# Image mix with its matrix as stationary, inside the value stage, turned through DRAM

## What is computed

```
xa = x.reshape(B * T, 1, H, W)          # after a group norm, 4 columns of W a group
xn = _inorm(xa, norm1_w, norm1_b)
k, q = (_fno_layer(xn, cw, sw, H // 2, W // 2) for cw, sw in ((Kcw, Ksw), (Qcw, Qsw)))
v = _fno_layer(xn, Vcw, Vsw, H, W)      # 32 heads: spectral part + pointwise skip
p_attn = softmax(scores(q, k))          # over the 32 images of a batch
av = einsum('bnts,bnsk->bntk', p_attn, v)
p = _fno_layer(av, Pcw, Psw, H, W)      # back to one head: spectral part + skip
a = _inorm(p + xa, attn_w, attn_b)
```

## Time and profile before

| what | us |
|---|---|
| median of 3 runs | 1873.72 (1869.31 to 1873.76) |
| the profiled execution | 1878.36 |
| its span, first to last instruction | 1876.6 |
| PE busy in the span | 1649.6 |
| DVE busy | 1484.6 |
| ACT busy | 1033.4 |
| POOL busy | 596.7 |

### The profile page before, as it was taken

How to read it: one execution, slowest core, us unless ns; L and a number is a source line. 1 busy time by engine, 2 the same in 40 slices (tenths; PEclk the granted TensorE clock), 3 DMA queues, 4 the chain that set the end, 5 groups by cost and what they waited for, 6 DMA issues and landing times.

```text
span 1876.6 us, 29918 instructions
## 1 busy us (share of the span) xinstructions
PE 1649.6 (88%) x11143; PEld 1018.5 (54%) x11143; DVE 1484.6 (79%) x2631; ACT 1033.4 (55%) x1544; POOL 596.7 (32%) x676
## 2 busy tenths in 40 slices
PE   7776878899889989389999999999999999999683
PEld 7751222699789989144444544445444454444342
DVE  5779999537766679889987998879988788884873
ACT  4379000133636155367777766677766776677620
POOL 2335878300256025424760130002280004000633
PEclk9897999999899999599999999999999999999897
DMA  6660363000000024000120021000132012000892
GB/s 159 252 163 23 93 151 87 8 1 1 1 1 2 1 72 116 3 1 1 23 57 1 13 34 34 12 1 23 24 80 57 1 57 62 7 12 19 296 377 104
DMA packets 132429, 114.03 MB, mean 61 GB/s; under 512 B 40384, under 2 KB 109376, under 8 KB 131744
## 3 DMA queue, kind: packets, MB, share of 16 engines
q1 hardware_dynamic: 128352, 108.00, 20.2%
q0 software_dynamic: 1536, 3.08, 0.5%
q10 hardware_dynamic: 2400, 1.03, 0.3%
HBM read 83.99 MB, written 21.88 MB: 56 GB/s over the span
## 4 chain that ended last, share of the span: by engine, by line
PE 67%; DVE 17%; issue 7%; ACT 6%; DMA 2%; POOL 1%; SPq 0%; POOLq 0%; DVEq 0%; ACTq 0%
PE PS L561 5%; PE PS L563 5%; PE PS L562 5%; PE PS L582 5%; PE PS L583 5%; PE PS L584 5%; PE PS L1467 5%; PE PS L1540 4%; PE PS L1549 4%; PE PS L543 4%; DVE U L1251 4%; PE PS L1700 3%; ACT Z L829 2%; DVE U L1308 2%; PE PS L531 2%
## 5 line engine op out<-in xcount | busy, mean ns | idle before, releaser
L826 ACT ACTIVATE Z<-PS,MI 128x1024 f32<-128x1024 f32 (+2 forms) x288 | 300.3, 1043 | 250.7 <-PE PS L563 221.3
L1033 DVE TENSOR_TENSOR DB<-Z 128x1024 f16<-128x1024 f32 (+2 forms) x288 | 333.4, 1158 | 100.9 <-ACT Z L829 51.7
L1013 DVE TENSOR_REDUCE MI<-PS 128x1 f32<-128x512 f32 (+2 forms) x576 | 356.8, 640 | 36.8 <-PE PS L543 20.2
L829 ACT ACTIVATE Z<-PS,MI 128x1024 f16<-128x1024 f32 (+2 forms) x288 | 298.5, 1037 | 0.0
L739 POOL TENSOR_SCALAR U<-U,Z 128x128 f32<-128x128 f32 x128 | 71.8, 576 | 323.0 <-DVE MI L1063 323.0
L756 POOL TENSOR_SCALAR Z<-U,Z 128x128 f32<-128x128 f32 x104 | 66.6, 652 | 338.9 <-PE PS L584 236.4
L1263 POOL TENSOR_TENSOR U<-A,U 128x1408 f32<-128x1408 f32 x45 | 142.3, 3209 | 42.6 <-PE PS L1672 22.1
L1251 DVE TENSOR_TENSOR U<-A,PS 128x1408 f32<-128x1408 f32 x99 | 152.9, 1616 | 3.3 <-PE PS L1666 3.2
L1672 PE MATMUL PS<-U 128*32 128x352 f32 x1152 | 112.7, 495 | 0.1
L582 PE MATMUL PS<-Z,A 128*128 128x512 f16 (+3 forms) x288 | 104.3, 362 | 6.2 <-ACT CST L837 6.2
L582 PE MATMUL PS<-Z,V 128*128 128x512 f16 (+3 forms) x288 | 104.0, 361 | 4.0 <-ACT CST L837 4.0
(11 more groups left out here) (437 smaller groups left out, 3595.1 us busy)
## 6 DMA issues: line engine op xcount, KB each, us to landing
V<-in_L_ffn_weight SPq DMA_DIRECT2D x16, 1024.0 KB, 11.4
U<-in_L_ffn_weight SPq DMA_DIRECT2D x14, 1024.0 KB, 14.6
A<-x_planes SPq DMA_DIRECT2D x24, 528.0 KB, 9.4
U<-in_x SPq DMA_DIRECT2D x16, 512.0 KB, 4.3
V<-in_x SPq DMA_DIRECT2D x4, 2048.0 KB, 14.0
Z<-in_x SPq DMA_DIRECT2D x16, 512.0 KB, 4.7
out<-U SPq DMA_DIRECT2D x16, 512.0 KB, 3.4
token_rows<-U SPq DMA_DIRECT2D x16, 512.0 KB, 3.9
```

Source lines behind the costliest of these rows:

```text
L826: act.activation(EX32[u % 2][:, 0:w], s, ACT.Exp, scale=SCALE / (QUP * KUP), bias=pb).then_inc(sem("ex_ev"), 1)
L829: act.activation(EHI[u % 3][:, 0:w], s, ACT.Exp, scale=SCALE / (QUP * KUP), bias=pb).then_inc(sem("hi_ev"), 1)
L1013: dve.tensor_reduce(bm[:, g % 2, t, k:k + 1], PS[:, 4 + chunk_no[c] % 2, 0:w], AX.X, ALU.max).then_inc(sem("ch_ev"), 1)
L1033: dve.tensor_tensor(ELO[u % 3][:, 0:w], EX32[u % 2][:, 0:w], EHI[u % 3][:, 0:w], ALU.subtract).then_inc(sem("lo_ev"), 1)
```

## The change

- The norm of `V` takes four columns (one group of the group norm, which has one scale) in an instruction.
- The planes of the value stage have one set of banks, 0 to 2. A row's first value matmuls wait for the sums of the row before it (`zv_ev` >= r), and VectorE makes these sums after group 0 of the new row instead of group 1.
- The image mix moves into the value stage. After each of the first 32 groups of VectorE, TensorE makes one `mix(g)`: `Mt` is stationary, 512 columns of `V` move, the result (image on the partition) goes to bank 3, 4 or 5. ScalarE copies it back over the same columns of `V`, and after every fourth copy issues a DMA of 2048 columns to the DRAM tensor `mixed`.
- SP loads `mixed` into `U` with h on the partition, 16 loads of eight images, three in flight, after all writes have landed and all value matmuls are done.
- TensorE's fold waits for `mx_ev` and `zv_ev` alone; the copies into `U` are gone. VectorE's additions in the first inverse wait for the load of their images. The semaphores of a later load of `x` take the new names, with counts shifted.

```diff
--- before.py
+++ after.py
...
@@ -1238,6 +1239,11 @@
                 dve.wait_ge(sem("fin_mm"), n + 1)
                 dve.tensor_tensor(token[q][k], token[q][k], PS[:, n % 8, 0:D], ALU.add).then_inc(sem("fin_ready"), 1)
 
+        MIX_BANKS = (3, 4, 5)
+        NMIX = 32
+        mixes_after = [min(d + 1, NMIX) for d in range(len(VALUES_DVE))]
+        row_ends = [sum(NDVS[:r + 1]) for r in range(NR)]
+
         def value_products(dve, d):
 
             r, g = VALUES_DVE[d]
@@ -1403,6 +1409,15 @@
                                  io[f"L0_conv_{n}"].rearrange("a b k x c -> (a b k) (x c)")).then_inc(sem("mw_in"), 16)
                 sp.dma_start(wrow[:, i], io[f"L0_conv_{n}"][0, :, :, 0, :]).then_inc(sem("mw_in"), 16)
 
+            sp.wait_ge(sem("mix_out"), 16 * NMIX // 4)
+            sp.wait_ge(sem("v_dve"), 3 * len(VALUES_DVE))
+            sp.wait_ge(sem("v_pool"), 3 * len(VALUES_POOL))
+            mix_nat = mix_dram.rearrange("n (h w) -> h n w", w=W)
+            for c in range(16):
+                if c >= 3:
+                    sp.wait_ge(sem(f"images_in{c % 3}"), 16 * (c // 3))
+                sp.dma_start(U[:, 8 * c:8 * c + 8, :], mix_nat[:, 8 * c:8 * c + 8, :]).then_inc(sem(f"images_in{c % 3}"), 16)
+
             sp.wait_ge(sem("tr_mm"), 3 * NTR)
             for i, n in enumerate("qkv"):
                 sp.dma_start(WN3[:, i, :], io[f"L1_attn_W{n}"]).then_inc(sem("l1w_in"), 16)
...
@@ -1669,37 +1684,37 @@
             def values(y, r, g, q, stop):
                 for b in range(B):
                     s = slice(32 * b, 32 * b + 32)
-                    mm = pe.matmul(PS[s, 3 * (r % 2) + q, 0:MR], PT[:, g, s], y[:, b, q, :], start=(g == 0), stop=stop)
+                    mm = pe.matmul(PS[s, q, 0:MR], PT[:, g, s], y[:, b, q, :], start=(g == 0), stop=stop)
                 return mm
+
+            def mix(g):
+                if g == 0:
+                    pe.wait_ge(sem("once_dve"), MADE["mt"])
+                    pe.wait_ge(sem("once_act"), BY_ACT_ONCE["xg"])
+                if g >= 3:
+                    pe.wait_ge(sem("mx_ev"), g - 2)
+                pe.matmul(PS[:, MIX_BANKS[g % 3], :], Mt, V[:, 512 * g:512 * g + 512], start=True, stop=True).then_inc(sem("mx_mm"), 1)
 
             spread(0)
             spread(1)
             p = -1
             for d, (r, g) in enumerate(VALUES_DVE):
                 p += g in POOL_BEHIND[NDVS[r]]
-                if g == 0 and r >= 2:
-                    pe.wait_ge(sem("zv_ev"), r - 1)
                 for q in range(3):
                     i = 3 * d + q
                     pe.wait_ge(sem("y_dve"), i + 1)
                     if i + 2 < 3 * len(VALUES_DVE):
                         spread(i + 2)
+                    if g == q == 0 and r:
+                        pe.wait_ge(sem("zv_ev"), r)
                     values(YB[d % 2], r, g, q, g == NDVS[r] - 1 and g not in POOL_BEHIND[NDVS[r]]).then_inc(sem("v_dve"), 1)
                     if g in POOL_BEHIND[NDVS[r]]:
                         pe.wait_ge(sem("y_pool"), 3 * p + q + 1)
                         values(YB[2], r, VALUES_POOL[p][1], q, g == NDVS[r] - 1).then_inc(sem("v_pool"), 1)
-            pe.wait_ge(sem("once_dve"), MADE["mt"])
-            pe.wait_ge(sem("once_act"), BY_ACT_ONCE["xg"])
-            xg = V[:].rearrange("p (h w) -> p h w", w=W)
-            for g in range(32):
-                if g >= 4:
-                    emptied(pe, "mx_ev", g - 4)
-                elif g == 0:
-                    pe.wait_ge(sem("zv_ev"), NR)
-                for j in range(4):
-                    mm = pe.matmul(PS[:, g % 4, 128 * j:128 * j + 128], xg[:, :, 4 * g + j], Mt, start=True, stop=True)
-                mm.then_inc(sem("mx_mm"), 1)
-            all_emptied(pe, "mx_ev", 1, 32)
+                for m in range(mixes_after[d - 1] if d else 0, mixes_after[d]):
+                    mix(m)
+            pe.wait_ge(sem("mx_ev"), NMIX)
+            pe.wait_ge(sem("zv_ev"), NR)
             pe.wait_ge(sem("once_dve"), MADE["wf"])
             for i in range(2):
                 for c in range(2):
@@ -1771,13 +1786,14 @@
 
             act.wait_ge(sem("once_dve"), MADE["rim"])
             act.wait_ge(sem("xi_in"), 64)
-            Vc = V[:].rearrange("p (h w) -> p w h", w=W)
+            Vc = V[:].rearrange("p (h w) -> p h w", w=W)
 
 
             def norm_columns(a, b):
 
-                for w in range(a, b):
-                    ins = act.activation(Vc[:, w, :], Vc[:, w, :], ACT.Identity, scale=rim[:, w:w + 1], bias=cim[:, w:w + 1])
+                for w in range(a, b, GW):
+                    x = Vc[:, :, w:w + GW]
+                    ins = act.activation(x, x, ACT.Identity, scale=rim[:, w:w + 1], bias=cim[:, w:w + 1])
                 return ins
 
             norm_columns(0, 96)
@@ -1789,14 +1805,25 @@
                 act.activation(PT[:, 4 * h:4 * h + 4, :].rearrange("p n s -> p (n s)"), PS[:, 2 + h, :], ACT.Copy).then_inc(sem("pt_ev"), 1)
             norm_columns(104, W).then_inc(sem("once_act"), 1)
             act.wait_ge(sem("x_out"), 48)
-            for r in range(NR):
-                act.wait_ge(sem("v_dve"), 3 * sum(NDVS[:r + 1]))
+
+            def first_plane(r):
+                act.wait_ge(sem("v_dve"), 3 * row_ends[r])
                 act.wait_ge(sem("v_pool"), 3 * sum(NQ - n for n in NDVS[:r + 1]))
-                act.activation(Z[:, 2, MR * r:MR * r + MR], PS[:, 3 * (r % 2), 0:MR], ACT.Copy).then_inc(sem("k1_ready"), 1)
-            Um = U[:].rearrange("p n w -> p w n")
-            for g in range(1, 32, 2):
+                act.activation(Z[:, 2, MR * r:MR * r + MR], PS[:, 0, 0:MR], ACT.Copy).then_inc(sem("k1_ready"), 1)
+
+            def mixed_out(g):
                 act.wait_ge(sem("mx_mm"), g + 1)
-                act.activation(Um[:, 4 * g:4 * g + 4, :], PS[:, g % 4, :].rearrange("p (w n) -> p w n", w=4), ACT.Copy).then_inc(sem("mx_ev1"), 1)
+                act.activation(V[:, 512 * g:512 * g + 512], PS[:, MIX_BANKS[g % 3], :], ACT.Copy).then_inc(sem("mx_ev"), 1)
+                if g % 4 == 3:
+                    act.wait_ge(sem("mx_ev"), g + 1)
+                    s = slice(512 * (g - 3), 512 * (g + 1))
+                    act.dma_start(mix_dram[:, s], V[:, s]).then_inc(sem("mix_out"), 16)
+
+            for d in range(len(VALUES_DVE)):
+                if d + 1 in row_ends:
+                    first_plane(row_ends.index(d + 1))
+                for m in range(mixes_after[d - 1] if d else 0, mixes_after[d]):
+                    mixed_out(m)
 
             def weigh_modes(layer):
 
@@ -2048,13 +2075,13 @@
                 dve.wait_ge(sem("k1_ready"), r + 1)
                 if r == 0:
                     dve.wait_ge(sem("x_out"), 48)
-                dve.tensor_tensor(Z[:, 0, m], Z[:, 2, m], PS[:, 3 * (r % 2) + 2, 0:MR], ALU.subtract)
-                later(dve.tensor_tensor(Z[:, 1, m], Z[:, 2, m], PS[:, 3 * (r % 2) + 1, 0:MR], ALU.add))
+                dve.tensor_tensor(Z[:, 0, m], Z[:, 2, m], PS[:, 2, 0:MR], ALU.subtract)
+                later(dve.tensor_tensor(Z[:, 1, m], Z[:, 2, m], PS[:, 1, 0:MR], ALU.add))
                 dve.tensor_scalar(Z[:, 2, m], Z[:, 0, m], -1.0, None, ALU.mult).then_inc(sem("zv_ev"), 1)
 
             for d, (r, g) in enumerate(VALUES_DVE):
                 value_products(dve, d)
-                if g == 1 and r:
+                if g == 0 and r:
                     value_sums(r - 1)
             value_sums(NR - 1)
 
@@ -2065,11 +2092,7 @@
             later(dve.tensor_tensor(wrow[:, :, neg, 0], wrow[:, :, neg, 0], wrow[:, :, pos, 0], ALU.add))
             later(dve.tensor_tensor(wrow[:, :, neg, 1], wrow[:, :, neg, 1], wrow[:, :, pos, 1], ALU.subtract))
             dve.memset(wrow[:, :, 0:32, :], 0.0).then_inc(sem("once_dve"), 1)
-            Um = U[:].rearrange("p n w -> p w n")
             dve.wait_ge(sem("z_ready"), 1)
-            for g in range(0, 32, 2):
-                dve.wait_ge(sem("mx_mm"), g + 1)
-                dve.tensor_copy(Um[:, 4 * g:4 * g + 4, :], PS[:, g % 4, :].rearrange("p (w n) -> p w n", w=4)).then_inc(sem("mx_ev0"), 1)
 
             def transposed_evacs(layer):
                 for g in range(0, NTR, 2):
@@ -2104,9 +2127,10 @@
             dve.wait_ge(sem("once_mm"), ONCE["fold"])
             later(dve.tensor_copy(WR[:, :, 0, :], PS[:, 5, 0:4].rearrange("p (l c) -> p l c", l=2)))
             dve.tensor_scalar(WN, WR[:, :, :, 1], -1.0, None, ALU.mult).then_inc(sem("once_dve"), 1)
-            all_emptied(dve, "mx_ev", 1, 32)
             transposed_evacs(0)
             for k in range(NIM):
+                if k % 2 == 0:
+                    dve.wait_ge(sem(f"images_in{k // 2 % 3}"), 16 * (k // 6 + 1))
                 dve.wait_ge(sem("i2_mm"), k + 1)
                 u = U[:, 4 * k:4 * k + 4, :]
                 dve.tensor_tensor(u, u, PS[:, 4 + k % 4, :].rearrange("p (n w) -> p n w", w=W), ALU.add).then_inc(sem("i2_ev"), 1)
```

(5 more changed lines are left out.)

## The result

| what | before | after |
|---|---|---|
| median, us | 1873.74 (1869.31 to 1875.64) | 1841.40 (1839.99 to 1842.94) |
| ratio, 95% interval | | 0.9831 [0.9811, 0.9851] |
| profiled execution, us | 1878.36 | 1840.46 |
| its span, us | 1876.6 | 1838.3 |
| value stage, first product to last sum, us | 169.0 | 195.3 |

The kernel became 32.3 us faster; 36.2 were forecast. The mix left the path as the prediction has it, and the value stage paid more for it than was forecast.

What follows compares the result with a forecast made beforehand. Stages follow one another: TensorE bounds the image mix and first inverse, VectorE the value stage. Terms -56.6 + 4 + 16.4 = -36.2 us give 1837.5 us against the median; range 1824 to 1857.

Steps and rivals of the forecast that it cites:

- mix off the path: Between last sum and fold: without the image mix the fold starts at 351.44 instead of 408.07, -56.6 us.
- mixes inside rows: Value stage: two mixes close together around a long group show about 0.37 us, twice in six rows, +4 us.
- row ends, beyond the 13.9 before: Five row ends: one plane set makes TensorE wait for VectorE's sums; 30.3 us against 13.9, +16.4 us.
- ways of the data, norm of V: Writes to DRAM, loads back and ScalarE's four-column norm steps: all hidden, 0 us.
- A mix at 0.86 us: TensorE in the value stage: one 512-column mix takes 0.86 us, or 1.08 if weight loads show.
- The 0.37 us behind a long group: Value stage: what shows when two mixes lie close together around a long group, twice in each of six rows.
- the hold: Row ends before rows 2 and 4: POOL's product holds up VectorE's last sum, 2.8 us more at each.
- Which clock at the row ends: TensorE behind the waits: low clock taken at all five ends; if only half fell, some 4 us cheaper.
- The data: Loads of mixed images into U: three in flight, 2.8 us each, hidden by 11 us at the narrowest.
- A: Value stage: TensorE catches up and keeps its clock, stage stays 169 us, mix goes under it; 1817 us, chance 0.10.
- B: Value stage: TensorE becomes the bound through weight loads, POOL's loads and low clock; 1855.5 us, chance 0.17.
- C: First inverse: images come back late from DRAM, one by one at 9.4 us a load; 1918 us, chance 0.06.

Runs made afterwards that it cites:

- run 6: Changed kernel with the 16 loads of mixed images one at a time instead of three in flight; 1841.89 us.
- run 2: Changed kernel with the 32 mixes placed elsewhere: four in TensorE's wait at each of five row ends, ten inside rows, two after the last row; 1820.65 us.
- run 4: Changed kernel with each mix matmul made twice, same operands and bank; 1866.13 us.
- run 5: Changed kernel with 16 matmuls of 128 columns, results unused, in TensorE's wait at each of five row ends; 1833.76 us.
- run 1: Kernel before with only one set of plane banks, its wait, and the sums after group 0; image mix in its old place; 1889.35 us.
- run 7: Changed kernel with the norm of V in 128 single columns as before; 1846.54 us.
- run 3: Changed kernel with VectorE's last sum made from PSUM, plane 2 minus plane 0, instead of a negated SBUF copy; 1837.15 us.

## Why the prediction was right, and where not

**The mix leaves the path: right.** The fold stands 1.14 us behind the last sum (375.88 to 377.02); 1.1 was forecast.

**The sum by its terms.** From the first product to the fold are 226.8 us before (181.30 to 408.07) and 196.4 after (180.58 to 377.02): -30.3 by the change, where the prediction has -36.2.

| term | predicted | measured |
|---|---|---|
| mix off the path | -56.6 | -56.6 |
| mixes inside rows | +4 | +6.2 |
| row ends, beyond the 13.9 before | +16.4 | +20.0 |
| ways of the data, norm of V | 0 | 0 |

The two middle terms were mis-sized, by 2.2 and 3.6 us; that is the whole miss up to the fold (but for 0.1 of rounding). The first is as large in run 6 (6.3 us), which has the same value stage. The second is not: from first product to fold run 6 takes 191.7 us instead of 196.4, and the difference lies at its row ends, 29.0 us instead of 33.9, where the clock fell less. That is 15.1 us beyond the 13.9, so the 16.4 of the forecast lies inside the scatter of this term. The median fell by 32.3 us, between the 30.3 of this execution and the 35.1 of run 6.

The profiled executions differ by 37.9 us, and some 7 of it lie behind the last addition into `U`: 1397.8 us from its end to the end of the span before, 1390.6 after, between 1390.1 and 1396.5 in the eight experiments. That is work which no edit here touches, but for the names of some semaphores, so I take it as scatter; this isn't shown. So it is luck that the profiled execution came so near to its forecast (1840.46 against 1842): these 7 us made up for the terms that were taken too low.

**A mix at 0.86 us: too low.** It takes 0.97 (187.17 to 188.14). The prediction had both ends, 0.86 and 1.08, and chose the lower since `Mt` lies contiguous. Back to back, four take 3.60 us (run 2); without the 0.16 by which a mix's row reaches past the next start (1.13 against 0.97) that is 0.86 each, as for a second mix with the same matrix (run 4). So 0.11 us more shows once for each mix that stands alone between other shapes, where I had weighed none or two; that it is a weight load is argued, not shown. The 0.37 us behind a long group became 0.54; it shows 11 times, and 0.25 once: 6.2.

**Row ends: the mechanism right, two steps too cheap.** The wait has the five places and the releaser that were forecast, and is somewhat shorter: 3.5 us at three ends and 5.5 with POOL at two, where about 4 and 7 were named. At the odd end above the first product is late by 4.39 us; the prediction's parts for it (1.24 + 0.14 + 2.51 + 0.51) make 4.4. Then I took 0.73 and about 0.6 us for the second product and the mix; the first is from the earlier trace rows, where the clock came back within the second batch. Here the second batch is slow to its end, and 1.23 and 1.00 show. The 1.00 is no price of the clock: it stands behind all three odd ends of run 5 too, where both batches are at full speed. It is the mix behind a long group that began late. At the even ends the hold is 2.58 us (2.8 taken), but the low clock lasts through three steps and into the mix: 1.73 us late there at the one, 1.15 at the other, instead of 0.7. That the hold came so near is in part luck: it is what is left of POOL's product at that moment, and the same two ends show 0.43 and 2.97 us in run 1, 0.99 and 0.96 in run 2. Sums: 6.6, 7.8, 5.6, 7.2 and 6.8 against 5.7, 6.6, 5.7, 6.6 and 5.7.

**Which clock at the row ends.** All five at the low one was right for this execution, and the trace agrees with the rule that I named from the Trainium skill ("TensorE: Matmul & The Clock Gate", Part 1) in direction. But it isn't certain for the odd ends: behind 3.5 us of idling the first sixteen matmuls ran slow at three of three odd ends in after, and at one of three each in runs 6 and 7, whose row ends are the same code. At one more end of each of these two the clock fell for the second sixteen, and at the third not at all. Where the first sixteen run fast the first product is 3.1 us late instead of 4.4. Behind 5.5 us the first batch was slow each time. How long TensorE idled doesn't decide it alone: in the kernel before the sixteen matmuls behind 1.87 and 2.62 us were slow, two rows which the prediction didn't use and which spoke for the low clock, and of those behind its two waits of 1.73 us one batch was:

```profile
221.20 0.31 PE L1666 MATMUL PS<-Z,ST 96*128 96x352 bf16 x1 [1.87 <-DVE U L1251]
221.44 2.54 PE L1672 MATMUL PS<-U 128*32 128x352 f32 x16
```

**The data: right.** The loads land every 1.9 us, not 2.8, from 380.68 to 408.94; the first is 11.3 us ahead of its addition (11 forecast). The writes delay nothing that can be seen: POOL is busy for 141.65 us (141.71 before), and none of its waits in the stage is put down to a load. Only the start of the loads was wrong: the prediction has it before the last sum, but the last write lands at 376.39, 0.5 us after that sum, and the loads begin then.

**The norm: right at 0, and it had a price if left out** (run 7). Its steps of four columns take 0.71 us where four old ones take 2.2:

```profile
176.99 4.33 ACT L1796 ACTIVATE V<-V,MI 128x512 f32<-128x512 f32 x6
```

`V` is ready at 181.3 instead of 190.8, and the first mix is due at 187.17.

**The rivals.** A (full cover, 1817) failed by the row ends above all (20.0 us, against 6.2 for the mixes inside the rows): with the wait filled the kernel takes 1820.65 us (run 2). B (TensorE the bound, 1855.5) did not come, but after stands near it: twice the mix shows 24.7 of 27.5 us (run 4). C fell by the landing times, and with run 6.

## What to carry to other kernels

Work that is moved under another engine's stage should go where its own engine waits there, not be spread evenly: the same 32 matmuls were worth 32 us one after each group and 53 us when a share of them filled the waits (some 3 us of that by the shorter hold). A buffer set that is given up is a new wait, and its price is the wait, plus the low clock behind it, plus whatever holds up the engine that releases it; the clock (run 5) and the hold (run 3) could each be taken away alone, the wait was filled in run 2 only together with both. The turn through DRAM was free here because the consumer starts late and takes the pieces slowly: compare landing times with due times, piece by piece, and look up whether a wait that a profile puts down to a load ends when the load lands.

## What the hardware showed that was not expected

- A wait of 2.7 us for `V` cost 3.6 us (run 7), and a hold of 2.6 us made even row ends 5.1 and 4.5 us dearer (run 3, from 7.8 and 7.2 to 2.66): in both the clock behind the wait took part of it.
- The 66 transposes behind the fold take 9.82 us in after, where TensorE idles for 3.09 us before the fold, and 8.40 in run 2, where it idles for 1.18. But the idling isn't what tells them apart: behind 1.16 us they take 9.82 in the kernel before and 8.40 in run 1, and TensorE's work there is the same. What decides stays open.

```profile
377.59 9.82 PE L1532 MATMUL PS<-CST,Z 128*128 128x128 f32 x66
```

```profile
408.64 9.82 PE L1517 MATMUL PS<-CST,Z 128*128 128x128 f32 x66
```

```profile
423.17 8.40 PE L1517 MATMUL PS<-CST,Z 128*128 128x128 f32 x66
```

- Useless matmuls in a wait made the kernel 7.6 us faster (run 5).
